# Query weights split once in the key and value stage, and loaded as ready parts by the grouped-query stage

## What is computed

```
q = norm(x) @ Wq          # (16*128, 1024) @ (1024, 32*128), then rotary position
k = ctx @ Wk;  v = ctx @ Wv   # 8 heads of 128, keys with rotary position
s = tanh(q.k * scale / 30) * 30;  p = exp(s) masked, divided by its sum
x = x + tanh(gate) * (p @ v) @ Wo
```

## Time and profile before

| what | us |
|---|---|
| median of 3 runs (3281.2 to 3283.25) | 3281.87 |
| the profiled execution | 3288.88 |
| its span, first to last instruction | 3287.1 |
| PE busy in it | 3080.6 (94%) |
| DVE busy | 2093.1 (64%) |
| POOL busy | 1851.3 (56%) |
| ACT busy | 1234.8 (38%) |
| mean granted TensorE clock, 1 is full | 0.969 |

### The profile page before, as it was taken

The page is one execution under the profiler, slowest core; times in us unless marked ns, Lnnn a source line. Parts: engine busy times, 40 slices in busy tenths (PEclk is TensorE's granted clock), DMA queues, the critical chain, the costliest instruction groups (busy, mean ns, idle before and its releaser), DMA issues. The chain is left out here.

```text
span 3287.1 us, 41110 instructions
## 1 busy us (share of the span) xinstructions
PE 3080.6 (94%) x14547; PEld 2474.0 (75%) x14547; DVE 2093.1 (64%) x2607; ACT 1234.8 (38%) x1898; POOL 1851.3 (56%) x1244
## 2 busy tenths in 40 slices
PE   7999679999999996899999999999999999998799
PEld 6888558788787775677777777777778787777577
DVE  3332357777777753767666767767777677676575
ACT  3111155555555541333333433433333434333222
POOL 4232354454454443667676767676767776764343
PEclk9999889999999997999999999999999999999799
DMA  7343501101111113222233222332222332323221
GB/s 200 107 131 109 180 26 39 65 33 65 53 45 65 52 54 114 102 90 102 89 128 141 102 95 96 121 147 96 96 96 101 129 134 96 111 90 134 84 71 52
DMA packets 171260, 315.53 MB, mean 96 GB/s; under 512 B 10328, under 2 KB 86488, under 8 KB 171144
## 3 DMA queue, kind: packets, MB, share of 16 engines
q1 hardware_dynamic: 171144, 314.04, 27.3%
HBM read 246.90 MB, written 67.11 MB: 96 GB/s over the span
## 5 line engine op out<-in xcount | busy, mean ns | idle before, releaser
L1850 DVE RECIPROCAL g_rsum<-pair 128x512 f32<-128x512 f32 x128 | 429.0, 3351 | 57.1 <-PE pair L1925 57.1
L1893 PE MATMUL pair<-g_xn_hi,g_wq_hi 128*128 128x512 f32 x1024 | 403.9, 394 | 19.1 <-POOL g_wq_lo L1569 14.0
L1893 PE MATMUL pair<-g_xn_lo,g_wq_hi 128*128 128x512 f32 x1024 | 402.5, 393 | 0.0
L1893 PE MATMUL pair<-g_xn_hi,g_wq_lo 128*128 128x512 f32 x1024 | 402.2, 393 | 0.0
L1949 PE MATMUL pair<-g_wo_hi,g_at_hi 128*128 128x512 f32 x992 | 389.6, 393 | 2.4 <-DVE g_res L1830 0.2
L1949 PE MATMUL pair<-g_wo_lo,g_at_hi 128*128 128x512 f32 x992 | 386.2, 389 | 0.0
L1949 PE MATMUL pair<-g_wo_hi,g_at_lo 128*128 128x512 f32 x992 | 386.1, 389 | 0.0
L1569 POOL TENSOR_TENSOR g_wq_lo<-g_wq_raw,g_wq_hi 128x1024 fp32r<-128x1024 f32 x130 | 310.9, 2415 | 0.0
L1569 POOL TENSOR_TENSOR g_at_lo<-g_at_raw,g_at_hi 128x512 fp32r<-128x512 f32 x128 | 180.1, 1407 | 217.6 <-ACT g_at_hi L1710 217.6
L1710 ACT ACTIVATE g_q_hi<-g_q_raw 128x512 fp32r<-128x512 f32 x128 | 81.0, 633 | 535.6 <-POOL g_q_raw L1650 535.6
L1810 DVE TENSOR_TENSOR g_q_raw<-pair,t_cos_q 128x512 f32<-128x512 f32 x128 | 88.5, 692 | 296.2 <-PE pair L1893 256.5
(11 more groups left out here) (251 smaller groups left out, 7333.3 us busy)
## 6 DMA issues: line engine op xcount, KB each, us to landing
g_wq_raw<-in_L_Wq SPq DMA_DIRECT2D x64, 1024.0 KB, 7.3
g_wo_raw<-in_L_Wo SPq DMA_DIRECT2D x62, 1024.0 KB, 6.3
values_split<-c_v SPq DMA_DIRECT2D x64, 256.0 KB, 2.8
keys_split<-c_k SPq DMA_DIRECT2D x32, 512.0 KB, 2.7
g_k<-keys_split SPq DMA_DIRECT2D x32, 512.0 KB, 3.2
g_v<-values_split SPq DMA_DIRECT2D x32, 512.0 KB, 7.7
c_cx_raw<-in_ctxT SPq DMA_DIRECT2D x16, 512.0 KB, 7.4
a_x<-in_x SPq DMA_DIRECT2D x16, 512.0 KB, 4.5
```

The lines of the kernel that those rows point to most:

```text
L1850: V.reciprocal(rsum[:, :], p_sum[:, :]).then_inc(rsum_done, 1)
L1893: mm = M(bank[:, :], w[a][:, i, cols], x[b][:, i, :], start=(i == 0 and t == 0), stop=(i == KT - 1 and t == 2))
```

## The change

The front stage gets a third task. The query weights are cut into 32 pieces r of 128 x 1024 (8 key heads by 4 pieces). Each piece is loaded, rounded by ScalarE, its low part made by POOL, and both parts are stored to a new scratch tensor `query_weights_split`. The pieces lie in heads 1 to 6: six slots to a head, one behind each of units 2 to 4 of the values and of the keys (`qp_at`). There are two buffers, and the load of a piece is issued behind the store of the piece before. The grouped-query stage loads the ready high and low parts, four loads of 1 MB a step instead of two, with 8 KB in a row; the splits on ScalarE and POOL fall away. The projection waits for the landing of each half of the weights, and at the turn of a group for all of the input's low parts. TensorE's loop takes the shape of the other engines' loops. The declarations, the semaphores and the arguments are left out:

```diff
...
     NPS = 4
+    QP, PW = 4 * NKV, 2 * BANK
     sb = Arena(nc, "c_", FLOOR)
...
     ident, ones = sb("ident", [P, P]), sb("ones", [P, P])
+    qp = []
+    for i in range(2):
+        qp.append({"lo": sb(f"qp{i}_lo", [P, PW], F32R), "hi": sb(f"qp{i}_hi", [P, PW], F32R),
+                   "raw": sb(f"qp{i}_raw", [P, PW], over=f"qp{i}_lo")})
     keep, cos_q, sin_q = kept_tiles
...
                 .then_inc(v_store[n % 2], 16)
+    def load_qp(r):
+        if r < QP:
+            after(sp, qp_store[r % 2], 32 * (r // 2))
+            sp.dma_start(qp[r % 2]["raw"].rearrange("p (a n) -> p a n", a=2), Wq_v[r // 4, r % 4])\
+                .then_inc(qp_land[r % 2], 16)
+    def store_qp(r):
+        sp.wait_ge(qp_lo, r + 1)
+        for i, part in enumerate(("hi", "lo")):
+            sp.dma_start(wq_out[r // 4, i, :, (r % 4) * PW:(r % 4 + 1) * PW], qp[r % 2][part][:, :].bitcast(F32))\
+                .then_inc(qp_store[r % 2], 16)
+    def pass_qp(j, unit):
+        for r in qp_at(j, unit):
+            store_qp(r)
+            load_qp(r + 1)
     A = nc.scalar.activation
+    def qp_round(j, unit):
+        for r in qp_at(j, unit):
+            act.wait_ge(qp_land[r % 2], 16 * (r // 2 + 1))
+            A(qp[r % 2]["hi"][:, :], qp[r % 2]["raw"][:, :], ACT.Copy).then_inc(qp_hi, 1)
     def round_hi(buf, view):
...
     G = nc.gpsimd
+    def qp_low(j, unit):
+        for r in qp_at(j, unit):
+            pool.wait_ge(qp_hi, r + 1)
+            low(G, qp[r % 2], lambda t: t[:, :]).then_inc(qp_lo, 1)
     def wv_low(q):
...
                     early["pool"][0]()
+                for i in range(3):
+                    qp_low(j, i)
                 for g in range(NGRP):
                     finish_k(j, g)
+                    if g > 0:
+                        qp_low(j, g + 2)
                     if j == NKV - 1 and 1 <= g < 3:
...
                 load_cx(b)
+            load_qp(0)
             for j in range(NKV):
...
                     store_v(j, i)
+                    if i > 0:
+                        pass_qp(j, i - 1)
                 if j == NKV // 2 - 1:
...
                 for g in range(NGRP):
+                    if j == NKV - 1 and g == 0:
+                        for i in range(2):
+                            sp.wait_ge(qp_store[i], 32 * QP // 2)
                     if j == NKV - 1 and g < 2:
...
                     store_k(j, g)
+                    if g > 0:
+                        pass_qp(j, g + 2)
                 if j + 1 < NKV:
...
                     v_round(j, i)
+                    if i > 0:
+                        qp_round(j, i - 1)
                     if j == 0:
...
                     k_round(j, g)
+                    if g > 0:
+                        qp_round(j, g + 2)
                     if j == NKV - 1 and g < 3:
...
             sp.dma_start(half(name, i)(buf["raw"]), half(name, i)(src)).then_inc(land[name][i], 16)
+    def load_wq(j):
+        for i in range(HALVES):
+            for s, part in enumerate(("hi", "lo")):
+                src = wq_in[:, s].rearrange("j p (k n) -> j p k n", k=KT)
+                sp.dma_start(half("wq", i)(wq[part]).bitcast(F32), half("wq", i)(one(src, j)))\
+                    .then_inc(land["wq"][i], 16)
     def load_acts(name, buf, src, g):
...
                 load_acts("xn", xn, xnT, z.g + 1)
-            load_halves("wq", wq, one(Wq_v, z.j_next))
+            load_wq(z.j_next)
             sp.wait_ge(s_done, FIRST + n * NB + NB)
...
             subtract_hi(nc.gpsimd, xn, part("xn", i, m)).then_inc(xn_lo, 1)
-    def wq_split(n, m):
-        pool.wait_ge(wq_hi, FIRST + n * 4 + m + 1)
-        subtract_hi(nc.gpsimd, wq, part("wq", m // 2, m % 2)).then_inc(wq_lo, 1)
     def wo_split(n, m, buf):
...
     def first_pool():
-        for done in (const_pool, xn_lo, wo_lo, rot_done, rot_lo, prob_lo, at_lo, wq_lo):
+        for done in (const_pool, xn_lo, wo_lo, rot_done, rot_lo, prob_lo, at_lo):
             pool.sem_inc(done, 1)
-        wq_split(0, 0)
     def first_low():
         xn_split(0, 0)
-        for m in range(1, 4):
-            wq_split(0, m)
     def body_pool(z):
...
             subtract_hi(nc.gpsimd, at, lambda t: t[:, :, bcols(b)]).then_inc(at_lo, 1)
-        early = not z.last and not z.group_end
         prob_split(0)
...
         prob_split(2)
-        if early:
-            wq_split(n + 1, 0)
-            wq_split(n + 1, 1)
         if z.group_end:
...
             xn_split(z.g + 1, 1)
-        if early:
-            wq_split(n + 1, 2)
-            wq_split(n + 1, 3)
         attn_split(2)
-        if z.group_end:
-            for m in range(4):
-                wq_split(n + 1, m)
         if z.last:
...
             quarters("xn", xn, z.g + 2, xn_hi, (2, 3))
-        if early:
-            quarters("wq", wq, n + 2, wq_hi, (0,))
         softmax(3)
-        if early:
-            quarters("wq", wq, n + 2, wq_hi, (1,))
         attn_hi(1)
         softmax_hi(3)
-        if early:
-            quarters("wq", wq, n + 2, wq_hi, (2, 3))
         attn_hi(2)
-        if z.group_end:
-            quarters("wq", wq, n + 2, wq_hi, range(4))
         if z.last:
...
         for i in range(KT):
-            if fresh is not None and i % 2 == 0:
-                pe.wait_ge(wq_lo, FIRST + 4 * fresh + i // 2 + 1)
+            if fresh is not None and i % (KT // HALVES) == 0:
+                pe.wait_ge(land["wq"][i * HALVES // KT], 32 * fresh + 32)
             for t, (a, b) in enumerate(SPLIT):
...
         return mm
-    def project(n):
+    def project(n, new_group=None):
+        if new_group is not None:
+            pe.wait_ge(xn_lo, FIRST + 2 + 4 * new_group)
         for h in range(G):
...
         values(n, 3)
+    def body_pe(z):
+        attend(z.n, first=z.first)
+        if not z.last:
+            project(z.n + 1, z.g + 1 if z.group_end else None)
     early = {"sync": (first_wq, first_xn), "act": (first_act, first_xn_hi), "pool": (first_pool, first_low),
...
             pe.wait_ge(const_act, FIRST + 2)
-            attend(0, first=True)
-            project(1)
-            with pe.Fori(1, last) as n:
-                attend(n)
-                project(n + 1)
-            attend(last)
+            steps(pe, body_pe)
             for u in range(NU):
...
```

More of the change, by code:

```diff
@@ L60, with key_value_stage @@
 SPLIT = (("hi", "hi"), ("hi", "lo"), ("lo", "hi"))
-def key_value_stage(nc, banks, kept_tiles, ctxT, Wk, Wv, mask, cos_t, sin_t, k_out, v_out):
+def key_value_stage(nc, banks, kept_tiles, ctxT, Wk, Wv, Wq, mask, cos_t, sin_t, k_out, v_out, wq_out):
     HD, NKV = 128, 8
@@ L115, in key_value_stage, with qp_at @@
     const_pool, const_dve, const_pe = sem("const_pool"), sem("const_dve"), sem("const_pe")
+    qp_land, qp_store = ([sem(f"{n}{i}") for i in range(2)] for n in ("qp_land", "qp_store"))
+    qp_hi, qp_lo = sem("qp_hi"), sem("qp_lo")
+    Wq_v = Wq.rearrange("(m a p) (j n) -> j m p a n", p=P, a=2, j=NKV)
+    def qp_at(j, unit):
+        r = 6 * (j - 1) + unit
+        return [r] if 1 <= j <= 6 and unit < 6 and r < QP else []
     def made_v(j, i):
@@ L1445, in linear_attention_moe_stage, with gqa_stage @@
     return Stage(early, run, sems)
-def gqa_stage(nc, banks, kept_tiles, x_in, xnT, k_in, v_in, gate, Wq, Wo, x_out):
+def gqa_stage(nc, banks, kept_tiles, x_in, xnT, k_in, v_in, gate, wq_in, Wo, x_out):
     HD, NH, NKV = 128, 32, 8
@@ L1497, in gqa_stage @@
     k_land, v_land = sem("k_land"), sem("v_land")
-    xn_hi, wq_hi, wo_hi = (sem(n + "_hi") for n in ("xn", "wq", "wo"))
-    wo_lo, wo_lo_dve, xn_lo, wq_lo = sem("wo_lo"), sem("wo_lo_dve"), sem("xn_lo"), sem("wq_lo")
+    xn_hi, wo_hi = (sem(n + "_hi") for n in ("xn", "wo"))
+    wo_lo, wo_lo_dve, xn_lo = sem("wo_lo"), sem("wo_lo_dve"), sem("xn_lo")
     xn_lo_dve = sem("xn_lo_dve")
@@ L1508, in gqa_stage @@
     at_hi, at_lo, y_done, y_added = sem("at_hi"), sem("at_lo"), sem("y_done"), sem("y_added")
-    Wq_v = Wq.rearrange("(k p) (j n) -> j p k n", p=P, j=NKV)
     Wo_v = Wo.rearrange("(j g p) n -> j p g n", p=P, j=NKV)
@@ L1588, in first_wq @@
     def first_wq():
-        load_halves("wq", wq, one(Wq_v, 0))
+        load_wq(0)
     def first_xn():
@@ L1723, in first_act @@
     def first_act():
-        for done in (const_act, xn_hi, wq_hi, wo_hi, rot_hi, tanh_done, exp_done, prob_hi, at_hi):
+        for done in (const_act, xn_hi, wo_hi, rot_hi, tanh_done, exp_done, prob_hi, at_hi):
             act.sem_inc(done, 1)
-        quarters("wq", wq, 1, wq_hi, range(4))
     def first_xn_hi():
@@ L2615, in flamingo_layers @@
     k_split, v_split = scratch("keys_split", (32, P, 2, BANK)), scratch("values_split", (32, P, 2, BANK))
+    wq_split = scratch("query_weights_split", (8, 2, P, KT * BANK))
     stack = ExitStack()
@@ L2620, in flamingo_layers @@
     kept_tiles = [top(n, [P, SEQ]) for n in ("keep", "cos_q", "sin_q")]
-    kv_sems, run_kv = key_value_stage(nc, banks, kept_tiles, a["ctxT"], a["L1_Wk"], a["L1_Wv"], a["mask"], a["cos"],
```

(5 more changed lines are left out.)

## The result

The change makes the kernel **slower by 2.8%**: 3374.61 us in the median (3373.97 to 3375.29, 4 runs), beside 3282.3 us of the kernel before on the same chip (3281.2 to 3283.25, 4 runs). The ratio is 1.0281, with a 95% interval of [1.0264, 1.0299]. Forecast were 3345 us and a range of 3298 to 3385. So the sign is right and the time lies in the range, but 30 us of the loss were not foreseen. The profiled execution took 3373.97 us, with a span of 3372.2 us.

A forecast was written before the change was run, and what follows sets the result against it. TensorE, busy 44.00 of 44.00 us, was taken to bound the front stage. Front-stage loss 84 + 1.5 - 22.7 gains = +62.8 on the profiled 3288.9 us, less 7.0 for the median: 3345 us, range 3298 to 3385.

The forecast's parts named there:

- round trip: Front stage, each piece: stores, load, rounding, low part in one chain on SP, 9.6 us (7.9 to 10.6).
- TensorE should idle before L292 and L306 for `emptied`: Front stage, expected sign: TensorE idles for this semaphore, a head takes some 61 us, the stage ends some 84 us later.
- the gate: End of front stage: piece 31 holds up the last key unit of head 6, which starts at 323.4 us.
- the trip was not covered: Rival, front stage: load passes the stores, lands 3.3 us after issue, trip 7.9, nothing lost, 3261 us; chance 0.14.
- the clock fell: Rival, front stage: TensorE's clock falls, hidden until its mean is below 0.71; at 0.5, 3482 us; chance 0.03.
- the turns gained: Rival, grouped-query stage: turns gain nothing, the projection waits as long for something else, 3364 us; chance 0.07.
- The gains: Grouped-query stage and passage into it: 6.2 us a turn, 18.7 for three, plus 4.0 at the passage; 22.7 us.
- the last normalisation: Passage into grouped-query stage: without three key low parts on POOL ahead, it goes 4.0 us sooner; bounds 0 and 4.
- Twice the loads: Grouped-query stage: four 1 MB loads a step take 10.4 us, 15.6 with new inputs, some 31 us ahead: cost 0.
- The nested loops: TensorE's one loop becomes nested loops: taken as 0, with 8 us as the other end.
- The length of the hand-overs: Front stage: 31 round trips 297.6 us, plus 30.5 for five changes of head and value weights at head 3: 328.
- The slack counted from the wrong start: Front stage: TensorE gives the trips 245.2 us, from second value unit of head 1 at 78.2 to 323.4.

The follow-up runs named there:

- e1_load_first: Changed kernel with the load of the next piece issued on SP ahead of the store of the piece before: 3300.55 us, ratio 1.0042.
- e4_stores_only: Changed kernel with 64 stores of ready context data, without wait; pieces' loads, roundings and low parts left out, wrong weights: 3260.96 us, ratio 0.9932.
- e8_all: Changed kernel, next load ahead, key weights' load before last piece, three slots free after value weights, POOL waiting for last stores, low parts on VectorE: 3285.53 us.
- e6_slots_off_value_weights: Best version: changed kernel, next load ahead, key weights' load before last piece, three slots free after value weights, POOL waiting for last stores: 3271.94 us.

## Why the prediction was right, and where it was short

**The mechanism** was the forecast one in its main part. A piece's load waits for the store before it on SP, pieces follow at the pace of a round trip, and TensorE, which needs 5.45 us for a unit, has no work to put in between. Exchanging the two lines, halving the pieces and shortening the trip in the order of the change all moved the time the way that says. The path from the trips to TensorE was forecast wrongly: "TensorE should idle before L292 and L306 for `emptied`". It idled for weights, 92.3 us at the first key unit of five heads and 10.3 us once for value weights, because their loads or splits stand behind a head's pieces. The trips set the length of a head either way, so the time depended on this only by the 4 us of the gate below. The rivals fall: the trip was not covered (the load lands 5.5 us after its own issue, not 3.3), the clock fell only around the waits (0.87 in the mean of the front stage, above the 0.71 that the rival named), and the turns gained. The four terms below all erred the same way, so the hit rests on the width of the range (3385 at its upper end), not on errors that cancel.

**The gains** were right: 6.4 to 6.6 us a turn against 6.2 (54.39, 54.72 and 54.54 us; before 60.76, 61.07 and 61.13), 3.9 us at the last normalisation (TensorE's idle before its last turns from 12.16 to 8.26) against 4.0. The 1.3 us of the stage's first step were not forecast. Within a group the step stayed at 53.2 us as forecast. Twice the loads cost nothing there: the 4 MB of a step are down 11 to 13 us after their first issue (15.2 to 16.4 at a turn; 10.4 forecast within a group), and the projection that needs them comes 31 us after it (26 to 28 at a turn). The nested loops cost nothing either.

**The front stage** came out 32.2 us longer than forecast (117.7 against 85.5). Four terms were too small; they add up to 32.1:

- *The length of the hand-overs*, "31 round trips are 297.6 us, with 30.5 they are 328": they sum to 345.2 us, 17.1 more. The ordinary trip is 9.98 us, not 9.6 (25 of them, 9.6 us in all). In the trip shown the load was down 6.38 us after the first store's issue, not 5.9, while the hops were cheaper. The change of head took 14.2, not 13.2 (five, 5 us in all), and the value weights 24.5, not 22.1. Of that 1.0 us 0.7 is POOL's: "in this stage rotation and value splits read PSUM" left out the key weight's low part, which VectorE makes from two inputs in SBUF. Six of the 32 pieces' low parts on POOL, the first one and those at the five changes of head, lie beside it and took 3.05 to 3.08 us, not 2.42.
- *The slack counted from the wrong start*, 8.3 us. The sum let the first piece be handed over when the second value unit was rounded, at about 80.3 us (67.28 + 10.9 + 1.5 + 0.6). It was handed over at 88.65. ScalarE's timeline of the kernel after, just before:

```profile
82.96 1.06 ACT L222 ACTIVATE c_wk_hi<-c_wk_raw 128x1024 fp32r<-128x1024 f32 x1 [6.58 <-DMA c_wk_raw<-in_L_Wk]
83.93 0.58 ACT L241 ACTIVATE c_v<-pair 128x512 fp32r<-128x512 f32 x1
84.41 1.06 ACT L219 ACTIVATE c_qp_hi<-c_qp_raw 128x1024 fp32r<-128x1024 f32 x1
```

  The same rounding in the kernel before:

```profile
81.04 1.06 ACT L187 ACTIVATE c_wk_hi<-c_wk_raw 128x1024 fp32r<-128x1024 f32 x1 [6.19 <-DMA c_wk_raw<-in_L_Wk]
```

  The key weight's load is issued at 77.67 us, and ScalarE's rounding of it stands ahead of the first piece. That lag was in the kernel before at every head (31.0 us in six waits for this load between 60 and 330 us) and used up slack that the 245.2 us counted as free. I had the five changes of head in the sum, but not the one at which the pieces begin.
- *The gate*, "the unit that piece 31 holds up is the last key unit of head 6". The unit that TensorE last waited for was the first key unit of head 6, at 421.98, for the key weight, whose load stands behind piece 29. Three units later is 438.3, 4.4 us behind the last hand-over of 433.89, where the sum had 0.5: 4 us more. The idle comes in one lump of 15.6 to 21.5 us a head instead of in small ones.
- *The clock* behind the last wait, 2.7 us. From 421.98 four units took 24.46 us instead of 21.8: behind 17.80 us of idle the clock was granted at 0.50, the lower level, until 427.5, and at 1.00 from there. Only the part behind the last wait counts in this sum. That the other 10.5 us of slower products were hidden in the trips, as the rival said they would be, follows from the chain; no run tests it.

What stays open is the front stage of the best version: it still ends 12.3 us later than before, with 7.5 us of new waits for weights in its trace; the rest was not followed up.

## What to carry to other kernels

Two buffers overlap nothing if the queue that issues the load first waits for the work on the buffer before it: write down, for each buffer, the ring of store, landing, load and split, divide by the number of buffers, and compare it with the time that the bounding engine gives each piece. When work is added to an engine or queue that runs in order, list what stands behind its new waits and which of these the bounding engine needs first; here that was a weight's load, not the stores of results. A step of such a ring that is made faster helps only while it is the step waited for: here, with the load first, the shorter low part was ready before its stores could be issued, and stores so close behind a load landed later.

## What the runs showed of the hardware that I had not expected

- *POOL slows down beside one form of VectorE's work.* The piece's low part took 2.40 us on POOL, but 3.06 us at 149.50, where VectorE made the key weight's low part (149.12 to 150.34, both inputs in SBUF). The Trainium skill (SBUF — State Buffer, "Who interferes with whom") says that such an instruction contends with POOL's reads, and that the port pair they share is locked exclusively. The overlap was 0.84 us, the delay 0.66, so the trace agrees. Beside a rotation, which reads PSUM, a low part still took 2.40 us (113.16 in `e1_load_first`, rotation from 112.16 to 114.26).
- *Stores of this size are nearly free for a bound TensorE.* 64 stores of 512 KB between 84 and 310 us moved the front stage's end by 2.7 us (`e4_stores_only`).
- *SP takes longer to issue a load right behind stores.* A piece's load took SP 0.39 us to issue with the load first (114.69), 0.72 directly behind two stores (109.71 in the changed kernel), and the key weight's load right behind that one 1.17 (140.12).
- *The closer stores follow a load, the later they land.* Two stores of 512 KB had landed 6.5 to 9.6 us after the first issue where they followed a load of 512 KB by 0.42 to 0.43 us (`e8_all`), and 4.5 to 6.0 us where they followed by 1.9 to 2.4 us (`e6_slots_off_value_weights`).
